# Reordered matmuls in the narrow expert tiles, two early expert loads and a shifted router step, in a fused attention and expert layer on one core

## The reference, cut to what matters

```python
xn = _layernorm(x)
x = x + attn_ref(xn, ...) + ffn_ref(xn, ...)

# attn_ref: time mixing, then channel mixing
x2 = x + sigmoid(mix @ Wr) * (einsum('bth,th->bh', xln @ Wv, dec)[:, None, :] @ Wo + bo)
kc = square(relu(shift(xc) @ Wck))        # 512 -> 2048
out = x2 + sigmoid(xc @ Wcr) * (kc @ Wcv) # 2048 -> 512

# ffn_ref: causal attention with 16 heads of 32, then 8 experts, 2 for each token
x = x + softmax(causal(q @ k.T * scale)) @ v @ Wo.T
logits = xn @ Wr.T;  top_logits, top_idx = top_k(logits, 2)
probs = softmax(top_logits)
y_e = (silu(xn @ Wg[e].T) * (xn @ Wu[e].T)) @ Wd[e].T   # 512 -> 1024 -> 512
out = x + sum over the token's two experts of prob * y_e
```

## Time and profile before

| | us |
|---|---|
| median of 3 runs | 1722.92 (1721.09 to 1723.02) |
| the profiled execution's own time | 1721.07 |
| its span (first to last instruction) | 1719.3 |
| PE busy | 1619.1 (94%) |
| VectorE (DVE) busy | 1015.2 (59%) |
| ScalarE (ACT) busy | 911.6 (53%) |
| GpSimd (POOL) busy | 482.1 (28%) |
| mean share of the DMA engines, turn of the experts' loop | 0.71 |

### The profile page before, as it was taken

How to read it: one execution, slowest core, us unless ns; L and a number is a source line. 1 busy time by engine, 2 the same in 40 slices (tenths; PEclk the granted TensorE clock), 3 DMA queues, 4 the chain that set the end, 5 groups by cost and what they waited for, 6 DMA issues and landing times.

```text
span 1719.3 us, 26079 instructions
## 1 busy us (share of the span) xinstructions
PE 1619.1 (94%) x9014; PEld 1348.1 (78%) x9014; DVE 1015.2 (59%) x1968; ACT 911.6 (53%) x1637; POOL 482.1 (28%) x647
## 2 busy tenths in 40 slices
PE   3978899999999999999999989999999999999996
PEld 2756678877777777777777879898989898989895
DVE  6787743127665565665546445757575756575652
ACT  6465654334555655555642235656565656565652
POOL 4353420100121212212120213333333424242422
PEclk9989999999999999999999999999999999999998
DMA  6354576889796876976586565768685858576762
GB/s 234 109 168 150 204 231 170 229 253 342 236 292 188 255 220 194 291 211 171 203 233 218 189 184 194 272 197 284 197 282 201 272 197 281 207 253 232 242 224 25
DMA packets 119795, 375.37 MB, mean 218 GB/s; under 512 B 30239, under 2 KB 30239, under 8 KB 105954
## 3 DMA queue, kind: packets, MB, share of 16 engines
q1 hardware_dynamic: 99426, 334.60, 58.0%
q0 software_dynamic: 15696, 31.21, 9.8%
q10 hardware_dynamic: 4592, 8.52, 1.3%
HBM read 292.62 MB, written 87.82 MB: 221 GB/s over the span
## 4 chain that ended last, share of the span: by engine, by line
PE 68%; DVE 4%; ACT 2%; DMA 2%; issue 2%; POOL 0%; DVEq 0%; ACTq 0%; SPq 0%; POOLq 0%
PE bank L53 15%; PE bank L54 15%; PE bank L55 15%; PE bank L2328 4%; PE bank L2366 4%; PE bank L2361 4%; PE bank L2362 4%; PE bank L2305 2%; PE bank L2293 2%; DVE ex_w_lo L2737 1%; PE bank L2840 1%; DVE hd_a L2105 1%; DMA hd_gate<-scratch_rc 1%; ACT hd_a_hi L1973 1%; PE bank L2400 1%
## 5 line engine op out<-in xcount | busy, mean ns | idle before, releaser
L2737 DVE TENSOR_TENSOR ex_w_lo<-ex_stage,ex_w_hi 128x1024 fp32r<-128x1024 f32 x207 | 248.7, 1236 | 175.1 <-ACT ex_w_hi L2647 166.8
L2573 POOL TENSOR_TENSOR ex_a_lo<-ex_a,ex_a_hi 128x256 fp32r<-128x256 f32 x128 | 92.6, 747 | 298.6 <-ACT ex_a_hi L2669 298.5
L53 PE MATMUL bank<-ex_x_hi_a,ex_w_hi 128*128 128x256 f32 x512 | 145.8, 285 | 4.0 <-DVE ex_a L2775 4.0
L55 PE MATMUL bank<-ex_x_hi_a,ex_w_lo 128*128 128x256 f32 x512 | 145.0, 283 | 0.0
L54 PE MATMUL bank<-ex_x_lo_a,ex_w_hi 128*128 128x256 f32 x512 | 144.9, 283 | 0.0
L53 PE MATMUL bank<-ex_x_hi_b,ex_w_hi 128*128 128x256 f32 x512 | 144.7, 283 | 0.0
L55 PE MATMUL bank<-ex_x_hi_b,ex_w_lo 128*128 128x256 f32 x512 | 144.3, 282 | 0.0
L54 PE MATMUL bank<-ex_x_lo_b,ex_w_hi 128*128 128x256 f32 x512 | 144.3, 282 | 0.0
L2165 DVE CUSTOM_DVE_ANT_0 hd_masked<-bank,causal 128x512 bf16<-128x512 f32 (+3 forms) x256 | 114.6, 485 | 34.9 <-PE bank L2293 34.2
L2644 ACT ACTIVATE ex_w_hi<-ex_stage 128x1024 fp32r<-128x1024 f32 x134 | 133.8, 1048 | 0.5 <-DMA ex_stage<-in_w_moe 0.5
L53 PE MATMUL bank<-ex_w_hi,ex_a_hi 128*128 128x512 f32 x312 | 126.2, 404 | 0.3 <-DVE ex_w_lo L2737 0.3
(11 more groups left out here) (325 smaller groups left out, 4480.1 us busy)
## 6 DMA issues: line engine op xcount, KB each, us to landing
ex_stage<-in_w_moe SPq DMA_DIRECT2D x69, 1536.0 KB, 7.0
first_w<-in_w_moe SPq DMA_DIRECT2D x23, 1536.0 KB, 7.0
hd_up<-scratch_up_halves SPq DMA_DIRECT2D x48, 512.0 KB, 6.7
st_qk<-scratch_qk SPq DMA_DIRECT2D x64, 256.0 KB, 4.9
hd_down<-scratch_down_halves SPq DMA_DIRECT2D x28, 512.0 KB, 5.9
hd_more_halves<-scratch_down_halves SPq DMA_DIRECT2D x20, 512.0 KB, 5.9
st_qk<-scratch_qk SPq DMA_DIRECT2D x128, 64.0 KB, 4.7
scratch_up_halves<-hd_up SPq DMA_DIRECT2D x16, 512.0 KB, 4.1
```

What stands on the lines that cost most here:

```text
L53: pe.matmul(out, lhsT=w_hi, rhs=x_hi, start=first, stop=False)
L55: return pe.matmul(out, lhsT=w_lo, rhs=x_hi, start=False, stop=last)
L2573: pool.tensor_tensor(a_lo[:, chunk.par, m, :], a[:, m, :], a_hi[:, chunk.par, m, :].bitcast(F32), ALU.subtract).then_inc(wide_lo_ready, 1)
L2737: return dve.tensor_tensor(dst, src, hi.bitcast(F32), ALU.subtract)
```

## The change

Five edits:

1. `pe_up_narrow` no longer uses `mm3`. It first runs the 8 matmuls that need only high weights, waiting for `ex_w_hi` alone, and then the 4 with low weights, waiting for `ex_w_lo` there.
2. `stage2` and `stage3` exchange their memory. Chunk 2 of the first tile is loaded as soon as the last up piece is done, ahead of the last two gate loads on SyncE's queue; chunk 3 is loaded by `experts.sync`. Chunk 1 stays where it was; its helper is now `load_first(sp, 1)`.
3. In `load_next_downs` SyncE waits only if there is something to load.
4. On VectorE `slots_on_dve` runs inside piece 123, between the last `hd_a` of the block and its `hd_a_lo`, where it ran ahead of that `hd_a`. The first part of it stands before, the rest (`columns_on_dve`) behind `hd_a_lo`.
5. `TURN_AT` is 132 and no longer 131: the first rows are turned behind the first down piece of the block, not ahead of it.

The number of gate places stays two.

```diff
-    OVER_STREAMS = ("stage2", "stage3", "a_hi")
+    OVER_STREAMS = ("stage3", "stage2", "a_hi")
...
-    TURN_AT = TABLE_AT + 3
+    TURN_AT = TABLE_AT + 4
...
                     first = ring_blocks.index(block) * DEEP + PLACES
-                    sp.wait_ge(sum_done, sums_before[k] + 1)
-                    for n in range(first, min(first + DEEP, len(ring_blocks) * DEEP)):
+                    last = min(first + DEEP, len(ring_blocks) * DEEP)
+                    if first < last:
+                        sp.wait_ge(sum_done, sums_before[k] + 1)
+                    for n in range(first, last):
                         load_half(ring_blocks[n // DEEP], n % DEEP)
...
-                    experts.load_second(sp)
+                    experts.load_first(sp, 1)
+                if ups_before[k] == ALL_UPS - 1 and order[k][0] == "up":
+                    sp.wait_ge(up_done, ALL_UPS)
+                    experts.load_first(sp, 2)
...
                 begin(k)
+                if k == count_at + 5:
+                    route.slots_on_dve(dve)
                 finish(k)
...
-                if k == count_at + 4:
-                    route.slots_on_dve(dve)
+                if k == count_at + 5:
                     route.columns_on_dve(dve)
-                if k == count_at + 5:
                     route.experts_on_dve(dve)
...
-    def load_second(sp):
+    def load_first(sp, c):
         e = sp.value_load(experts[0:1, 0:1], min_val=0, max_val=E - 1)
-        sp.dma_start(stage[1][:, :], d["w_moe"][e * C + 1]).then_inc(stage_in[1], 16)
+        sp.dma_start(stage[c][:, :], d["w_moe"][e * C + c]).then_inc(stage_in[c], 16)
...
-        e = sp.value_load(experts[0:1, 0:1], min_val=0, max_val=E - 1)
-        for c in range(2, C):
-            sp.dma_start(stage[c][:, :], d["w_moe"][e * C + c]).then_inc(stage_in[c], 16)
+        load_first(sp, 3)
...
     def pe_up_narrow(pe, chunk):
         hi, lo = x_hi[NARROW], x_lo[NARROW]
-        pe.wait_ge(wu_lo_ready, (chunk.g + 1) * len(UP_PARTS))
+        pe.wait_ge(wu_hi_ready, (chunk.g + 1) * len(UP_PARTS))
         pe.wait_ge(a_full, (chunk.g - 1) * CK + (1 if chunk.c == 0 else 0))
...
         for k in range(HC):
-            last = mm3(pe, up_bank[chunk.par][:, :].rearrange("p (u n) -> p u n", u=2), hi[:, k, :], lo[:, k, :],
-                       both(w_hi, k), both(w_lo, k), k == 0, k == HC - 1)
+            pe.matmul(bank, lhsT=hi[:, k, :], rhs=both(w_hi, k), start=(k == 0), stop=False)
+            pe.matmul(bank, lhsT=lo[:, k, :], rhs=both(w_hi, k), start=False, stop=False)
+        pe.wait_ge(wu_lo_ready, (chunk.g + 1) * len(UP_PARTS))
+        for k in range(HC):
+            last = pe.matmul(bank, lhsT=hi[:, k, :], rhs=both(w_lo, k), start=False, stop=(k == HC - 1))
         last.then_inc(up_done, CK)
```

More of the change, by code:

```diff
@@ L2460 @@
 Programs = namedtuple("Programs", (
-    "load_second", "sync", "prepare_gpsimd", "gpsimd", "first_weights_scalar", "first_rows_scalar", "scalar",
+    "load_first", "sync", "prepare_gpsimd", "gpsimd", "first_weights_scalar", "first_rows_scalar", "scalar",
     "first_weights_vector", "first_rows_vector", "vector", "first_rows_tensor", "first_tensor", "tensor"))
@@ L2861, in pe_up_narrow @@
         hi, lo = x_hi[NARROW], x_lo[NARROW]
-        pe.wait_ge(wu_lo_ready, (chunk.g + 1) * len(UP_PARTS))
+        pe.wait_ge(wu_hi_ready, (chunk.g + 1) * len(UP_PARTS))
         pe.wait_ge(a_full, (chunk.g - 1) * CK + (1 if chunk.c == 0 else 0))
+        bank = up_bank[chunk.par][:, :].rearrange("p (u n) -> p u n", u=2)
         def both(w, k):
@@ L2937, in tensor @@
             pe_step(pe, chunk, LAST)
-    return Programs(load_second, sync, prepare_gpsimd, gpsimd, first_weights_scalar, first_rows_scalar, scalar,
+    return Programs(load_first, sync, prepare_gpsimd, gpsimd, first_weights_scalar, first_rows_scalar, scalar,
                     first_weights_vector, first_rows_vector, vector, first_rows_tensor, first_tensor, tensor)
```

## The result

| | before | after |
|---|---|---|
| median, us | 1722.01 (1720.89 to 1723.02, 4 runs) | 1706.28 (1703.46 to 1706.88, 4 runs) |
| ratio | | 0.9906, 95% interval 0.9888 to 0.9923 |
| span of the profiled execution | 1719.3 | 1705.1 |
| its own time | 1721.07 | 1706.88 |

A forecast was written before the change was run, and what follows sets the result against it. PE, busy 94% of the span, was taken as the bound. Terms of 6.4 + 5.0 + 1.1 + 0.8 = 13.3 us off the span of 1719.3 gave 1706.0, as a median 1709.6 us, range 1706.5 to 1716.5.

The forecast's parts named there:

- What bounds the kernel: Whole kernel: PE is busy 94% of the span, so time is won only where PE stands or runs at half clock.
- Narrow tiles: Experts' loop, last narrow chunk: PE's wait for low weights goes, 0.91 us in each of 7 turns, 6.4 us gained.
- it starts 0.91 us earlier: Last narrow chunk of a turn: PE starts at 1091.45 instead of 1092.36, no longer waiting for low weights.
- 6.4 above, since there is no more wait to take: Upper bound for the narrow tiles' gain: at most 6.4 us, all the idle time shown there.
- Weight loads: Rival in the narrow tiles: 112 added loads of 188 ns not hidden, 21.1 us lost, 1730.7 us; chance 0.03.
- Chunk 2: First tile: earlier load cuts PE's stop from 4.01 to 0.63 us and removes half clock; 3.38 + 1.65 = 5.0 us.
- The late gates: Rival ahead of the first tile: gate loads queue behind chunk 2, VectorE 7.2 us late, 1718.5 us; chance 0.07.
- Router and transposes: Router's slots behind `hd_a` gain 1.1 us, with new waits for `hd_acc`; first rows' transposes one piece later gain 0.8 us.

The follow-up runs named there:

- load_only: The kernel before with only the first tile's chunk 2 loaded behind the last up piece and chunk 3 behind the gates; 1715.65 us in one execution.
- new_order_old_wait: The changed kernel, keeping the new order of narrow matmuls but waiting for the low weights ahead of all of them; 1716.96 us, ratio 0.9967.
- lanes_later: The changed kernel with both of VectorE's steps that make `rt_lane_hit` one piece later; 1703.15 us in one execution, 1705.87 us when timed again.
- router_only: The kernel before with only the router's slots moved inside piece 123, between `hd_a` and `hd_a_lo`; 1719.58 us in one execution.

## Why the prediction was right, and where it was wrong

**What bounds the kernel** was right: all that was won was PE's standing and half clock, and the number of matmuls and loads didn't move.

**Narrow tiles: the mechanism right, the size wrong.** The wait left, didn't move to the low matmuls, and nothing else took its place. The failed step is "it starts 0.91 us earlier": the idle time in brackets was taken as the price of the stop. The term came out at 8.83 / 7 = 1.26 us a turn and not 0.91. The missing 0.35 us are in the earlier trace rows and in the rows of after. The trace counts idle time from the modelled end of the matmul before, which is 0.39 us long, but the next could have started at the pitch of 0.23 us. This is the last matmul ahead of the stop in the trace of before:

```profile
1091.06 0.39 PE L55 MATMUL bank<-ex_w_hi,ex_a_lo 128*128 128x512 f32 x1
```

Its successor was due at 1091.29 and came at 1092.36: 1.07 us. Then the first pitch behind the stop is 1092.70 - 1092.36 = 0.34 us instead of 0.23: 0.11 more. That is 1.18. By starts of chunks, the one before to the last narrow one is 5.50 us in before and 4.41 in after, and from there to the next wide one 4.52 and 4.39: 1.09 + 0.13 = 1.22. The rest varies from one execution to another: with the stop a turn takes 88.93 to 88.95 us or 89.06 (before has both, `load_only` 88.93 throughout), without it 87.73 each time. Over the six kernels with the old wait the seven turns' stretch is 628.03 to 628.51, so the stop's price is 1.20 to 1.27 us, and why a turn has one length or the other is open. `new_order_old_wait` shows that nothing but the stop is in it. The stop of 1.40 us that `lanes_later` takes away follows the same working: in the changed kernel the last start ahead of it is 948.54 (948.08 and two pitches), the next was due at 948.77 and came at 950.33, and the first pitch is 0.31 instead of 0.23: 1.56 + 0.08 = 1.64, and 1.62 were measured. The surplus also overturns the bound "6.4 above, since there is no more wait to take", which is why the range ended too early.

**Weight loads.** The rival of 1730.7 was wrong: the pitch is 0.23 us with no two matmuls sharing rows, and `new_order_old_wait` costs at most 0.1 us against before in its stretch (628.51 and 628.43), where the rival had 21.1. The Trainium skill, "TensorE: Matmul & The Clock Gate", section "Step-by-step: what each phase is for", has PE pull a load ahead under a running matmul; with a fresh load for every matmul of the narrow up passes, and no idle time before any of them, this trace agrees.

**Chunk 2** was right in every place on its chain, within 0.15 us, and the clock with it: 3.56 + 1.66 = 5.22 against 3.38 + 1.65. The 0.18 us more is for the most part ScalarE's: it starts chunk 2 7.09 us behind the first expert matmul, where the forecast's place is 7.25 behind; why isn't shown. What the forecast lacked is that the stop before was no constant: 4.01, 2.61, 3.40 and 5.43 us in four kernels with the old loads, and the stretch with it 69.74, 66.54, 69.39 and 72.06. Against the 64.5 of the new order that is a gain of 2.0 to 7.5 us by the execution. The one that I priced it by happened to be near the middle (4.9 on the mean of the four), so that the size came out within 0.2 us is in part luck.

**The late gates** did appear, 0.70 us, but the wait is the second load's and doesn't hang on the mechanism named (the queue behind chunk 2), since `router_only` has it with no weight load in front; and it cost 0. The Trainium skill, "DMA: Bandwidth & Descriptors", section "Queues, rings and completion order", has descriptors of one ring consumed in order. The first gate load agrees with that: it took 3.1 to 4.2 us with chunk 2 ahead of it and 2.6 or 2.7 without. Loads that share the engines' rate would look the same, and no run here separates the two.

**Router and transposes** came out at 1.00 and 0.66 us for 1.1 and 0.8, with the waits for `hd_acc` that were foretold. That the half clock would go without coming back behind the short stops was the value taken, and held in all nine traces with edit 4: stops like 1.07, 0.45 and 1.40 us left the clock at 1.00 there.

**The base.** The prediction went from a median of 1722.92 in 3 runs; over the runs of this study the kernel before had medians from 1721.4 to 1722.3, and one single execution of 1721.3. 1709.6 less 0.9 for that and 2.4 for the narrow tiles is 1706.3, which was measured; the small errors of the other terms cancel.

## What to carry to other kernels

Price a stop of PE by starts, not by the idle time in brackets: from the last start plus one pitch to the next start, and add what the first pitch behind it is longer; a stop shown as 0.91 us was worth 1.20 to 1.27 (1.18 by this rule), and one of 1.40 was worth 1.62 (1.64). Price a stop that a load ends from several executions: one and the same was 2.6 to 5.4 us long. Where a product is made in several passes, the pass whose operand is ready first can be run first at no cost, so long as the pitch doesn't hang on sharing the stationary side. And judge a small edit by the stretch between two instructions that both kernels have: the place at which the edits begin moved by up to 5 us from one kernel's execution to another's.

## What the hardware showed beside

Stops of PE from 900 us on and the clock granted behind them: half clock appeared behind stops of 3.12, 3.14, 3.40, 4.01 and 5.43 us, none behind those of 2.61, 1.53, 1.40, 1.10 or 0.91. So the same late load cost half clock in three executions and none in a fourth. But the length alone doesn't decide, as one stop early in the kernel shows, ahead of all edits. In the kernel before and then in the changed one, PE's row and the stretch behind it:

```profile
194.35 2.01 PE L863 MATMUL bank<-ident,tm_t 128*128 128x128 f32 x12 [2.51 <-ACT tm_x L493]
195.20:198.60 3.40, 3.40 (x12) 2.46 (x11) 0.17 (x1) 2.89 (x9) 0.15 (x1) 0.50 0.00 0
195.45 1.80 PE L863 MATMUL bank<-ident,tm_t 128*128 128x128 f32 x14 [2.48 <-ACT tm_x L493]
195.50:200.00 4.50, 4.50 (x23) 2.95 (x24) 0.17 (x1) 3.70 (x11) 0.45 (x1) 1.00 0.00 0
```

The stop is 2.51 and 2.48 us long; one execution has half clock behind it and the other not. What decides isn't shown. The last gate load, 128x512 float32, issued at 1001.14, was awaited until 1006.60, 5.5 us; over the 13 traces it landed 3.7 to 5.7 us after its issue, and why that varies is open. Whether the surplus of a stop is the same for all lengths was tried at these two lengths alone.
